# Attention and block-selection kernel: the first norm starts on fewer constants, and its bias and weight preparation is rearranged

## What is computed

```python
x = x + _L0_conv_ref(_gn(x), ...)      # windowed attention, then a feed-forward part
x = x + _L1_conv_ref(_gn(x), ...)      # top-k pixels of 8x8 blocks, a small network, spread back

def _gn(v, G=32, eps=1e-05):           # as called: 32 groups along the last axis
    g = v.reshape(B_, H_, W_, G, C_ // G)
    m = jnp.mean(g, axis=(1, 2, 4), keepdims=True)
    s = jnp.var(g, axis=(1, 2, 4), keepdims=True)
    return ((g - m) / jnp.sqrt(s + eps)).reshape(v.shape)

scores = scores / jnp.clip(tau, 0.01)[None, :, None, None]
bias = jax.nn.relu(_REL @ meta_w1 + meta_b1) @ meta_w2 + meta_b2      # per pair of tokens and head
bias = bias.T.reshape(HEADS, TOK, TOK)
scores = scores + bias[None]
```

## Time and profile before

| what | value |
|---|---|
| median of 3 runs | 783.17 us |
| lowest and highest run | 781.18, 783.38 us |
| span of the profiled execution (first to last instruction) | 778.6 us |
| that execution's own total time | not given apart from its span |
| busy share PE / DVE / ACT / POOL | 86% / 66% / 62% / 46% |
| mean granted TensorE clock over the span | 0.923 |
| HBM read and written | 20.71 and 9.37 MB |

### The profile page before, as it was taken

How to read it: one execution, slowest core, us unless ns; L and a number is a source line. 1 busy time by engine, 2 the same in 40 slices (tenths; PEclk the granted TensorE clock), 3 DMA queues, 4 the chain that set the end, 5 groups by cost and what they waited for, 6 DMA issues and landing times. The chain is left out here.

```text
span 778.6 us, 21192 instructions
## 1 busy us (share of the span) xinstructions
PE 665.7 (86%) x8584; PEld 371.4 (48%) x8584; DVE 516.4 (66%) x997; ACT 480.4 (62%) x963; POOL 355.1 (46%) x441
## 2 busy tenths in 40 slices
PE   4785789999999999999998579999999988749880
PEld 2562455565565555655555232233333367735350
DVE  4796487877777787877778322577777786372181
ACT  3565266777777777777775548877777656624000
POOL 4696446778777777788776520022221123100000
PEclk9787599999999999999999959999999999969955
DMA  9550000000000000000000020122112220120278
GB/s 216 137 128 11 1 3 2 3 2 3 2 3 3 3 3 3 3 2 3 3 2 3 2 56 1 28 55 56 33 50 55 55 55 2 31 72 2 63 194 269
DMA packets 15719, 31.44 MB, mean 40 GB/s; under 512 B 7488, under 2 KB 9284, under 8 KB 15620
## 3 DMA queue, kind: packets, MB, share of 16 engines
q1 hardware_dynamic: 12592, 29.16, 14.1%
q10 hardware_dynamic: 2760, 0.66, 0.5%
q0 software_dynamic: 272, 0.27, 0.2%
HBM read 20.71 MB, written 9.37 MB: 39 GB/s over the span
## 5 line engine op out<-in xcount | busy, mean ns | idle before, releaser
L794 POOL TENSOR_TENSOR sc<-sc,mx 128x512 f32<-128x512 f32 x128 | 133.7, 1044 | 102.4 <-DVE mx L725 102.4
L722 DVE TENSOR_TENSOR sc<-s_ps,bias_tab 128x512 f32<-128x512 f32 x128 | 87.7, 685 | 52.6 <-PE s_ps L528 52.6
L1424 POOL TENSOR_TENSOR square<-xs 128x1024 f32<-128x1024 f32 x16 | 34.1, 2133 | 165.5 <-DVE xs L1166 165.5
L539 PE MATMUL t_ps<-consts,sc 128*128 128x128 f32 x512 | 84.4, 288 | 16.2 <-ACT pt L656 12.5
L656 ACT ACTIVATE pt<-t_ps 128x512 f32<-128x512 f32 x128 | 75.7, 592 | 31.2 <-PE t_ps L539 30.1
L539 PEld LDWEIGHTS t_ps<-consts,sc 128*128 128x128 f32 x512 | 54.3, 142 | 84.8 <-issue 48.1
L725 DVE TENSOR_REDUCE mx<-sc 128x8 f32<-128x512 f32 x128 | 87.8, 686 | 4.4
L1081 ACT ACTIVATE hs<-h_ps,fb1s 128x512 f32<-128x512 f32 x128 | 78.2, 689 | 19.1 <-PE h_ps L990 19.0
L528 PE MATMUL s_ps<-kx,qu 32*64 32x128 f32 x2048 | 72.3, 278 | 3.5 <-DVE kx L749 2.9
L990 PE MATMUL h_ps<-xs,fw 64*128 64x512 f32 x256 | 68.7, 650 | 1.0 <-ACT hs L1081 1.0
L528 PEld LDWEIGHTS s_ps<-kx,qu 32*64 32x64 f32 x2048 | 56.7, 134 | 15.2 <-issue 13.4
(11 more groups left out here) (207 smaller groups left out, 1295.2 us busy)
## 6 DMA issues: line engine op xcount, KB each, us to landing
raw<-in_x_dram SPq DMA_DIRECT2D x32, 256.0 KB, 5.1
xr<-in_x_dram SPq DMA_DIRECT2D x32, 256.0 KB, 3.9
out_dram<-x SPq DMA_DIRECT2D x32, 256.0 KB, 3.9
...
```

The lines of the kernel that those rows point to most:

```text
L539: last = pe.transpose(t_ps[:, m], sc[n % KEPT][:, m].rearrange("c h k -> c (h k)"), ident)
L722: dve.tensor_tensor(sc[n % KEPT][:, :, :, :], s_ps[j][:, :, :, :], bias_tab[:, j, hp], ALU.add)\
L794: pool.tensor_tensor(v, v, mx[n % KEPT][:, :].unsqueeze(2).broadcast_to([128, 8, TOK]), ALU.subtract)\
```

## The change

The constants are cut to 128 x 544 and come in two loads: `sum_image` and `spread_image` (256 columns) first, the rest between the x loads of pairs 1 and 2. ScalarE makes `mean_group` and `mean_image` with two scaled copies. TensorE enters the norm when these are made; the two meta matmuls stand behind its steps 0 and 1, Relu and the bias by distance behind ScalarE's steps 1 and 2, and the eight column copies in pairs behind its steps 3 to 6. The spreading to full rows is gone: SP stores the eight column selections (4 x 960 values) behind its last x load, waits for the store, and reads the table with 16 transfers, one for each half and query row, each to 8 partitions. The bias by distance shares the bank of the hidden values, and the second exponential gets two banks of its own. VectorE's preparation is cut in three, behind its steps 14, 15 and 16, TensorE's part goes behind its step 15.

```diff
--- before.py
+++ after.py
@@ -80,10 +80,9 @@
...
         xs = flat[:, LEAD:].rearrange("c (p n) -> c p n", p=PAIRS)
-        consts = sb(whole, "consts", [128, 6 * 128 + 2 * DH])
-        ident, sum_image, spread_all, spread_even, spread_odd, spread_image = (
-            consts[:, 128 * n:128 * (n + 1)] for n in range(6))
-        sum_heads = consts[:, 6 * 128:]
+        consts = sb(whole, "consts", [128, 4 * 128 + 2 * DH])
+        sum_image, spread_image, ident, spread_all = (consts[:, 128 * n:128 * (n + 1)] for n in range(4))
+        sum_heads = consts[:, 4 * 128:]
         ones = sum_image[:, C - DH:C + DH]
...
...
@@ -262,12 +262,11 @@
...
             by_dist = sb(stage, "by_dist", [HEADS, SPAN, SPAN])
-            by_dy = sb(stage, "by_dy", [HEADS, SPAN, WS, WS])
-            bias_rows = sb(stage, "bias_rows", [HEADS, WS, WS, WS, WS])
+            by_dy = sb(stage, "by_dy", [HEADS, WS, SPAN, WS])
             hid_ps = ps(stage, "hid_ps", [128, COLS])
-            bias_ps = ps(stage, "bias_ps", [128, COLS])
+            bias_ps = hid_ps[0:HEADS, 256:256 + SPAN * SPAN]
             bp_ps = hid_ps
-            rstd_ps = ps(stage, "rstd_ps", [128, COLS])
+            rstd_ps = [ps(stage, f"rstd_ps{k}", [128, COLS]) for k in range(2)]
...
@@ -284,49 +283,53 @@
...
-            n1, gn_run, gn_v, gn_t, gn_a, gn_p = group_norm(stage, raw, xu, x_arrives, [bias_ps, rstd_ps])
-            def bias_tensor(pe):
+            n1, gn_run, gn_v, gn_t, gn_a, gn_p = group_norm(stage, raw, xu, x_arrives, rstd_ps)
+            def bias_hidden(pe):
+                pe.wait_ge(meta_in, 16 * len(meta_loads))
+                pe.matmul(hid_ps[:, 0:SPAN * SPAN], mw1[:, :], rel[:, :], start=True, stop=True)\
+                  .then_inc(hid_ps_ready, 1)
+            def bias_output(pe):
                 pe.wait_ge(hid_ready, 1)
-                pe.matmul(bias_ps[0:HEADS, 0:SPAN * SPAN], mw2[:, :], hid[:, :], start=True, stop=True)\
-                  .then_inc(bias_ps_ready, 1)
-            def bias_scalar(act):
+                pe.matmul(bias_ps, mw2[:, :], hid[:, :], start=True, stop=True).then_inc(bias_ps_ready, 1)
+            def hidden_relu(act):
                 act.wait_ge(hid_ps_ready, 1)
                 act.activation(hid[:, :], hid_ps[:, 0:SPAN * SPAN], ACT.Relu, bias=mb1[:, 0:1]).then_inc(hid_ready, 1)
+            def bias_by_distance(act):
                 act.wait_ge(bias_ps_ready, 1)
-                act.activation(by_dist[:, :, :].rearrange("h y x -> h (y x)"), bias_ps[0:HEADS, 0:SPAN * SPAN],
-                               ACT.Identity, bias=mb2[:, 0:1]).then_inc(by_dist_ready, 1)
-                act.wait_ge(by_dist_ready, 1)
-                for qx in range(WS):
-                    first = WS - 1 - qx
-                    last = act.activation(by_dy[:, :, qx], by_dist[:, :, first:first + WS], ACT.Copy)
-                last.then_inc(by_dy_ready, 1)
-            def bias_spread(act):
-                act.wait_ge(by_dy_ready, 1)
-                for qy in range(WS):
-                    first = WS - 1 - qy
-                    last = act.activation(bias_rows[:, qy].rearrange("h x v u -> h v x u"),
-                                          by_dy[:, first:first + WS], ACT.Copy)
-                last.then_inc(bias_rows_ready, 1)
-                act.wait_ge(bias_rows_ready, 1)
-                act.dma_start(bias_dram, bias_rows[:, :, :, :, :].rearrange("h q x v u -> h (q x v u)"))\
-                   .then_inc(bias_out, 16)
-            def bias_load(act):
-                act.wait_ge(bias_out, 16)
+                act.activation(by_dist[:, :, :].rearrange("h y x -> h (y x)"), bias_ps, ACT.Identity, bias=mb2[:, 0:1])\
+                   .then_inc(by_dist_ready, 1)
+            def bias_by_column(act, qx):
+                if qx == 0:
+                    act.wait_ge(by_dist_ready, 1)
+                first = WS - 1 - qx
+                act.activation(by_dy[:, qx], by_dist[:, :, first:first + WS], ACT.Copy).then_inc(by_dy_ready, 1)
+            def bias_columns(first):
+                return lambda act: [bias_by_column(act, qx) for qx in (first, first + 1)]
+            def bias_rows(sp):
+                by_column = bias_dram[:, 0:WS * SPAN * WS]
+                sp.wait_ge(by_dy_ready, WS)
+                sp.dma_start(by_column, by_dy[:, :, :, :].rearrange("h x d u -> h (x d u)")).then_inc(bias_out, 16)
+                sp.wait_ge(bias_out, 16)
                 for lo, hi in HALVES:
-                    act.dma_start(bias_q[lo:hi], bias_dram.rearrange("h (q k) -> q h k", k=TOK)).then_inc(bias_in, 16)
+                    for qy in range(WS):
+                        first = WS * (WS - 1 - qy)
+                        sp.dma_start(bias_q[lo + WS * qy:lo + WS * (qy + 1)],
+                                     by_column.rearrange("h (x n) -> x h n", x=WS)[:, :, first:first + TOK]).then_inc(bias_in, 16)
...
-            WP_READY = 12
+            WP_READY = 10
...
@@ -340,22 +343,27 @@
...
                 def _(sp):
-                    sp.dma_start(consts[:, :], c_consts).then_inc(consts_in, 16)
+                    sp.dma_start(consts[:, 0:256], c_consts[:, 0:256]).then_inc(image_in, 16)
                     for p in range(PAIRS):
+                        if p == 2:
+                            sp.dma_start(consts[:, 256:], c_consts[:, 256:]).then_inc(consts_in, 16)
                         after(sp, n1["first_half"], p - RING + 1)
...
                             sp.dma_start(raw[lo:hi, p % RING], x_pairs[a, :, p]).then_inc(x_in[p % RING], 16)
+                    bias_rows(sp)
...
                         act.dma_start(dst, src).then_inc(meta_in, 16)
-                    act.wait_ge(meta_in, 16 * len(meta_loads))
-                    bias_scalar(act)
-                    act.wait_ge(chain, 4)
-                    gn_run(act, gn_a, {2: bias_spread, 5: bias_load})
+                    act.wait_ge(image_in, 16)
+                    act.activation(mean_group[:, :], sum_image, ACT.Copy, scale=1.0 / (C * H)).then_inc(means_ready, 1)
+                    act.activation(mean_image, sum_image, ACT.Copy, scale=1.0 / C).then_inc(means_ready, 1)
+                    act.wait_ge(chain, 2)
+                    gn_run(act, gn_a, {1: hidden_relu, 2: bias_by_distance, 3: bias_columns(0), 4: bias_columns(2),
+                                       5: bias_columns(4), 6: bias_columns(6)})
...
@@ -378,36 +386,37 @@
...
                     link(dve.memset(eps[:, 1:2], NORM_FLOOR))
-                    dve.wait_ge(consts_in, 16)
-                    link(dve.tensor_scalar(mean_image, sum_image, 1.0 / C, None, ALU.mult))
-                    link(dve.tensor_scalar(mean_group[:, :], sum_image, 1.0 / (C * H), None, ALU.mult))
-                    def prepare(dve):
+                    def prepare_attention(dve):
+                        dve.wait_ge(consts_in, 16)
                         weights_there(dve)
...
                         link(dve.tensor_reduce(parity[:, :], heads_of[:, :].rearrange("c (g h) -> c h g", h=2), X, ALU.add))
+                    def prepare_projection(dve):
                         link(dve.tensor_reduce(small[:, 0:1], pw[:, :], X, ALU.add))
...
                         assert links[0] == WP_READY
+                    def prepare_bias(dve):
                         dve.wait_ge(bp_mean, 1)
...
-                    gn_run(dve, gn_v, {3: prepare})
+                    gn_run(dve, gn_v, {14: prepare_attention, 15: prepare_projection, 16: prepare_bias})
...
                 def _(pe):
-                    pe.wait_ge(meta_in, 16 * len(meta_loads))
-                    pe.matmul(hid_ps[:, 0:SPAN * SPAN], mw1[:, :], rel[:, :], start=True, stop=True)\
-                      .then_inc(hid_ps_ready, 1)
-                    pe.wait_ge(chain, 4)
-                    bias_tensor(pe)
-                    gn_run(pe, gn_t, {3: prepare_tensor})
+                    pe.wait_ge(image_in, 16)
+                    pe.wait_ge(means_ready, 2)
+                    gn_run(pe, gn_t, {0: bias_hidden, 1: bias_output, 15: prepare_tensor})
...
@@ -730,7 +739,7 @@
...
                     dve.tensor_copy(spread_half[rows(g), g % 2], spread_image[rows(g)])
-                dve.wait_ge(bias_in, 32)
+                dve.wait_ge(bias_in, 16 * 2 * WS)
                 for j in range(2):
...
@@ -1775,9 +1784,8 @@
...
     same = (half[:, None] == rows[None, :] // C) & (head[:, None] == rows[None, :] % C // DH) & (copy[:, None] == 0)
-    spreads = [same, same & (head[:, None] % 2 == 0), same & (head[:, None] % 2 == 1),
-               (half[:, None] == rows[None, :] // C) & (rows[:, None] % DH == 0)]
-    spreads = [a.astype(np.float32) for a in spreads]
+    same = same.astype(np.float32)
+    first = ((half[:, None] == rows[None, :] // C) & (rows[:, None] % DH == 0)).astype(np.float32)
     part = rows[0:2 * DH]
...
```

5 lines of the change are left out of this document (3 added, 2 removed).

## The result

| | median | lowest to highest | runs |
|---|---|---|---|
| before | 782.17 us | 780.86 to 783.38 | 4 |
| changed | 774.32 us | 772.55 to 775.53 | 4 |

The ratio is 0.9898, with a 95% interval of 0.9871 to 0.9924: 8.0 us faster, between 5.9 and 10.1. The forecast was 774.0 us in a range of 770.9 to 777.9. The spans of the two profiled executions, 778.6 and 773.7 us, differ by only 4.9 us. The profiled execution of the changed kernel was the slowest of its four, 775.53 us.

The account below looks back on a forecast made before the run. In the first norm TensorE sets the step at its lower clock, VectorE at the higher. Gains 3.2 + 2.9 + 2.9 + 0.4 − 0.2 = 9.2 us take the span from 778.6 to 769.4; plus 4.6 gives 774.0 us, range 770.9 to 777.9.

Parts of the forecast that it names:

- the hole: Step 3 of the first norm: VectorE idles while ScalarE spreads and stores bias rows; removing that work gains 2.9 us.
- the preparation: VectorE's weight preparation leaves step 3 of the norm, gain 2.9 us; placed behind steps 14 to 16 it costs 0.2.
- signs named: Trace signs of a right forecast: preparation behind pair 15's `centred`, no long VectorE idling, bias table without DMA wait, stated times.
- serial read-backs: Rival: the 16 bias-table transfers run one by one, holding the table until 131 us; 844 us in total, chance 0.02.
- a closed port for the moved scaling: Rival: GpSimd shuts out VectorE's spread_keys behind step 14 for 5.00 us; 778.5 us in total, chance 0.04.
- a low clock throughout: Rival: TensorE stays at 1.2 GHz through the norm, 12 steps at 2.91 us; 777.9 us in total, chance 0.08.
- late read-backs: Rival: SP's read-backs take 1.2 us an issue, ending at 64 against 61 us; 777.0 us in total, chance 0.04.
- meta matmuls that fill TensorE's holes: Rival at the norm's start: meta matmuls fit TensorE's waits, pair 3 at 17.7 us; 772.5 us in total, chance 0.14.
- Rival 6: At the norm's start, x alone sets the pace, pair 3 no earlier than about 21 us; 775.8 us, chance 0.03.
- The start: First norm up to pair 3's `centred`: 19.2 us instead of 22.43, gain 3.2 us, bounds 2.2 and 5.3.
- The pace: 12 norm steps behind pair 3: one at 2.9 us, 11 at 2.55; gain 0.4, bounds loss 0.8, gain 1.2.
- The level: Whole-kernel time: span 769.4 us plus the 4.6 us by which before's median 783.17 exceeds its span, giving 774.0.

Follow-up runs that it names:

- the last: Changed kernel with first meta matmul and Relu ahead of the norm, second behind TensorE's step 7, weight and second constants loads later: 771.15 us, ratio 0.9868.

## Why the prediction was right, and where it was not

**What was right.** As far as the rows tell, the change works in the first norm alone, the hole and the preparation go, the moved preparation costs nothing at the end, the read-backs are hidden, the loads of x never bind behind pair 2. Two of the signs named came out: pair 15's `centred` before the preparation, the table without a wait. The times named with them didn't: pair 3 near 19 (20.64), pair 15 near 50 (53.06), GpSimd's end near 57.7 (60.57), the table near 61 (63.55). Of the rivals, serial read-backs (0.30 us each to issue) and a closed port for the moved scaling (0.29 us) fell, and so did a low clock throughout (steps of 2.45 at the end), late read-backs (the last issue ends near 50.8) and meta matmuls that fill TensorE's holes (pair 3 at 20.64, not 17.7). Rival 6, pair 3 no earlier than about 21, had the size of the start nearly right. Its reason, x alone, holds only in part, since with the meta matmuls elsewhere pair 3 came at 18.66. Of the Trainium skill's two rules, the 2.0 us of fixed cost for a transfer ("DMA: Bandwidth & Descriptors", anatomy of a DMA) did not add up over the 16. The page measured it for transfers that GpSimd issues. One by one behind the first issue at 45.4, the 16 of SP would have held the table until about 77; it started at 63.55 without a wait, so the costs overlapped. The exclusion of VectorE and GpSimd ("SBUF — State Buffer", the two separate sides) would explain 4.79 against 0.23 us only in part, as the last section says, and beside GpSimd's placings the moved scaling took 0.29 us, so no wait of note appeared.

**What was not.** The stage gave 6.6 us, not 9.2.

*The start:* 3.2 forecast, 1.8 measured, and 1.8 to 2.0 when undone. That lies outside the term's own bounds of 2.2 to 5.3. The lower one was added up wrongly: matmuls of 1.1 us each take off 0.7 and pair 2 landing no sooner 0.6, which makes 1.9. Both sizes failed that way. I let the meta matmuls delay the means by 0.75 us each; they took 1.1 and 0.9. And I let pair 2 land 0.6 us sooner, at 12.5, by the bytes dropped; it landed at 13.5 against 13.1 before. Why 128 KB less ahead of it brought nothing wasn't found. The 0.6 us are less than what its arrival varies by (13.0 to 14.6), and GpSimd's loads run among those of x: with them and the second constants later it lands at 10.7.

*The pace:* the 12 steps from pair 3 were to take 31.0 us, and took 32.4. With the 5.8 us of hole and preparation taken off, they took 31.4 before, so this is a loss of 1.0 where a gain of 0.4 was forecast, beyond the bound of 0.8 too. The step that failed is "with no idle stretch TensorE should not fall back as it did from 28 to 37 us". It fell back for 10 us while almost fully busy. And I let one step behind pair 3 run at the low clock, where three did. Those three took 8.7 us instead of 8.0, the next five 13.9 instead of 12.8, and the last four 9.8 instead of 10.2. Wherever the stage stands in time, these 12 steps took 31.5 to 32.7 us in all runs without the hole or the preparation and 33.1 in the last. The 2.55 us a step came from a stretch of before that was better than the 2.7 that the changed kernel's 12 steps average.

*The hole and the preparation:* 5.8 us were forecast. Their step before was 8.35 us, and one like it after takes 2.8 to 2.9, which makes 5.5. Undone one at a time they cost 4.0 and 2.8 at the table, since together they overlapped by about 1.3 us.

*The level:* the time was still met, and that is luck. The stage gave 2.6 us less than the forecast 9.2. But before's median is 782.17 in the result, 1.0 below the 783.17 that the forecast starts from, and the medians differ by 7.9 us where the stage gave 6.6. The other 1.3 us lie behind the stage, where one profile differs from another by up to 8.3, and no run shows them to be the change's. The span says the same: 769.4 was forecast and 773.7 measured, and the 4.6 us put on top were 1.8 in every run (775.53 − 773.7), so the two errors cancel.
